# First attention of a two-layer model: 256-column score and value products in three float32r passes, single key/value buffers, normalisation and query parts on GpSimd

## What is computed

```python
# x: 4 x 256 x 256, normalised first; 16 heads of 128
q = (x @ Wq + bq).reshape(b, h, t, dh)
k = (x @ Wk + bk).reshape(b, t, h, dh).transpose(0, 2, 3, 1)
v = (x @ Wv + bv).reshape(b, t, h, dh).transpose(0, 2, 1, 3)
logits = jnp.einsum('bhtd,bhds->bhts', q, k) * scale
mask = jnp.triu(jnp.full((t, t), -jnp.inf, dtype=x.dtype), k=1)
weights = jax.nn.softmax(logits + mask, axis=-1)
out = jnp.einsum('bhts,bhsd->bhtd', weights, v)
out = out.transpose(0, 2, 1, 3).reshape(b, t, h * dh)
return out @ Wo + bo
```

## Time and profile before

| what | value |
|---|---|
| median of 3 runs | 483.01 us (482.86 to 483.03) |
| the profiled execution | 482.84 us |
| its span, first to last instruction | 481.1 us |
| busy: TensorE, VectorE, ScalarE, GpSimd | 456.8, 287.8, 212.8, 56.8 us |
| granted TensorE clock, mean | 1.000 |
| the loop over the units, first scores to the first work after it | 91.67 to 288.55 us |

### The profile page before, as it was taken

How to read it: one execution, slowest core, us unless ns; L and a number is a source line. 1 busy time by engine, 2 the same in 40 slices (tenths; PEclk the granted TensorE clock), 3 DMA queues, 4 the chain that set the end, 5 groups by cost and what they waited for, 6 DMA issues and landing times.

```text
span 481.1 us, 8091 instructions
## 1 busy us (share of the span) xinstructions
PE 456.8 (95%) x2946; PEld 389.0 (81%) x2946; DVE 287.8 (60%) x851; ACT 212.8 (44%) x554; POOL 56.8 (12%) x93
## 2 busy tenths in 40 slices
PE   3999999899999999999999899999998899999997
PEld 2788888698989889898998779999986646658897
DVE  5646574657676667676666547576888753544111
ACT  3454631356565665656555765333161242241100
POOL 3050000000000000000000000111650189200000
PEclk9999999999999999999999999999999999999999
DMA  6910520101010100100000000000899089900011
GB/s 188 227 45 1 176 72 17 44 1 46 0 45 3 43 2 16 30 1 1 1 1 1 2 1 0 1 1 1 280 283 278 3 233 294 256 1 2 0 42 46
DMA packets 40439, 32.32 MB, mean 67 GB/s; under 512 B 6432, under 2 KB 38864, under 8 KB 40400
## 3 DMA queue, kind: packets, MB, share of 16 engines
q1 hardware_dynamic: 40400, 31.80, 23.9%
HBM read 30.75 MB, written 1.05 MB: 66 GB/s over the span
## 4 chain that ended last, share of the span: by engine, by line
PE 83%; DVE 7%; ACT 5%; issue 3%; POOL 1%; DMA 1%; ACTq 0%; DVEq 0%; POOLq 0%
PE bank L779 15%; PE bank L780 15%; PE bank L781 15%; PE bank L947 5%; PE bank L929 5%; PE bank L1154 4%; PE bank L936 4%; PE bank L948 3%; PE bank L928 2%; PE bank L1126 2%; PE bank L1085 2%; PE bank L1146 2%; PE bank L1192 2%; PE bank L1191 2%; PE bank L1189 1%
## 5 line engine op out<-in xcount | busy, mean ns | idle before, releaser
L617 ACT ACTIVATE arena<-arena,nmax 128x128 f32<-128x128 f32 x64 | 25.7, 402 | 77.6 <-DVE nmax L1356 77.0
L779 PE MATMUL bank<-XTl,WA 128*128 128x512 f32 x128 | 54.2, 423 | 3.0 <-POOL WA L480 1.7
L780 PE MATMUL bank<-XTh,WA 128*128 128x512 f32 x128 | 51.4, 402 | 0.0
L781 PE MATMUL bank<-XTh,WA 128*128 128x512 f32 x128 | 51.3, 401 | 0.0
L497 POOL TENSOR_TENSOR arena<-arena 128x256 f32<-128x256 f32 x20 | 16.6, 857 | 266.8 <-ACT arena L680 247.2
L947 PE MATMUL bank<-arena 128*128 128x256 f32 x128 | 39.5, 391 | 1.1 <-ACT arena L626 1.1
L1345 DVE COPY arena<-bank 128x512 f32<-128x512 f32 x32 | 22.1, 691 | 30.6 <-PE bank L781 30.6
L1342 DVE TENSOR_SCALAR arena<-bank,VC 128x512 f32<-128x512 f32 x32 | 23.8, 749 | 24.9 <-PE bank L781 24.9
L779 PE MATMUL bank<-WA,XTh 128*128 128x256 f32 x128 | 38.3, 299 | 0.0
L929 PE MATMUL bank<-arena 128*128 128x256 f32 x128 | 38.2, 380 | 0.0
L780 PE MATMUL bank<-WA,XTl 128*128 128x256 f32 x128 | 35.7, 279 | 0.0
(11 more groups left out here) (273 smaller groups left out, 1193.7 us busy)
## 6 DMA issues: line engine op xcount, KB each, us to landing
arena<-in_L_ffn_Wg SPq DMA_DIRECT2D x6, 704.0 KB, 8.6
arena<-in_L_ffn_Wu SPq DMA_DIRECT2D x6, 704.0 KB, 10.4
arena<-in_L_ffn_Wd SPq DMA_DIRECT2D x6, 512.0 KB, 8.4
arena<-in_L_attn_Wq SPq DMA_DIRECT2D x4, 512.0 KB, 6.9
arena<-in_L_attn_Wk SPq DMA_DIRECT2D x8, 256.0 KB, 2.8
arena<-in_L_attn_Wv SPq DMA_DIRECT2D x8, 256.0 KB, 3.3
arena<-in_L_attn_Wo SPq DMA_DIRECT2D x1, 2048.0 KB, 9.6
arena<-in_L_ffn_Wd SPq DMA_DIRECT2D x6, 192.0 KB, 7.9
```

The costliest lines, as they stand in the source:

```text
L617: nc.scalar.activation(Pb[i][:, 0:128], Pb[i][:, 0:128], ACT.Exp, bias=nmax[:, i, 0:1], scale=-1.0, accum_out=psumr[:, i, 0:1])
L779: pe.matmul(dst, wh, xl, start=start, stop=False)
L780: pe.matmul(dst, wl, xh, start=False, stop=False)
L781: return pe.matmul(dst, wh, xh, start=False, stop=stop)
```

## The change

The 256-column score product and the 256-column value product go through `mm3`; the two 128-column ones stay f32. For this, keys and values are kept as a high part, a low part and a plain f32 part (`KH`, `KL`, `KP`, `VH`, `VL`, `VP`), and as these take more room there is one place for each instead of two. The fills of a pair come in another order (`FILL`, with the last quarter of the keys at the end), and six are done ahead instead of eleven. Waits on keys and values are counted per piece (`KC`). A key fill is emptied by ScalarE (`key_high`, 512 columns) and two VectorE passes, a value fill by three VectorE passes. The transposed probabilities are copied by ScalarE in two pieces and get a low part on VectorE (`t_low`). VectorE keeps the reciprocal (`inverse_sums`); the multiplications go to GpSimd (`normalise`), which also splits the 128 queries that see 256 keys (`query_parts`). Pieces of Wo and of the output projection move to later turns, and the split outputs get a place more (`o_place`). The diff, cut to its core:

```diff
-WO_AT = [16, 19, 22, 26, 53, 55, 57, 59]
-O_AT = {56: 0, 58: 2, 62: 1}
+WO_AT = [16, 19, 22, 26, 58, 59, 60, 61]
+O_AT = {58: 0, 61: 2, 62: 1}
+FILL = (0, 1, 2, 4, 5, 6, 7, 3)
+KC = {f: i + 1 for i, f in enumerate(FILL)}
...
-AHEAD = 11
+AHEAD = 6
...
-        KT = KTf.rearrange("p (a h n) -> p a h n", a=2, h=2)
+        KP = region(20480, 1024).rearrange("p (h b n) -> p h b n", h=2, b=B)
+        KH, KL = (nc.alloc_sbuf_tensor_at(f"K{i}", [P, 2, N], FR, offset=at0 + 4 * (21504 + 2048 * i)) for i in range(2))
         XN = KTf[:, 0:2048].rearrange("p (j d) -> p j d", j=NT)
-        WXA = KTf[:, 2048:4096].rearrange("p (j d) -> p j d", j=NT)
+        WXA = [region(28672 + D * j, D) for j in range(6)] + [region(32768 + D * j, D) for j in range(2)]
-        V = Vf.rearrange("p (a j n) -> p a j n", a=2, j=NT)
+        VH, VL = (nc.alloc_sbuf_tensor_at(f"V{i}", [P, B, 2 * DH], FR, offset=at0 + 4 * (25600 + 1024 * i)) for i in range(2))
+        VP = region(27648, 1024).rearrange("p (b n) -> p b n", b=B)
...
-        PTb = region(29440, 768).rearrange("p (i n) -> p i n", i=2)
+        PTH, PTL = (nc.alloc_sbuf_tensor_at(f"PT{i}", [P, 2, T], FR, offset=at0 + 4 * (29440 + 512 * i)) for i in range(2))
+        PTP = region(30464, 256).rearrange("p (i n) -> p i n", i=2)
+        QH, QL = (nc.alloc_sbuf_tensor_at(f"Q{i}", [P, 2, P], FR, offset=at0 + 4 * (30720 + 256 * i)) for i in range(2))
...
+        OSX = nc.alloc_sbuf_tensor_at("OSX", [P, 2, H // 2, P], FR, offset=at0 + 4 * 16384)
+        def o_place(n):
+            if n == 0:
+                return OSX
+            while n > 4:
+                n = {5: 2, 6: 1, 7: 3}.get(n, n - 4)
+            return OS[:, {2: 1, 1: 0, 3: 3, 4: 2}[n]]
...
+            def query_parts(u):
+                _, _, b, h = unit(u)
+                q = QO[:, h, b, 128:256]
+                if u >= 2:
+                    pool.wait_ge(s_S, u - 1)
+                pool.tensor_copy(QH[:, u % 2], q).then_inc(s_q1, 1)
+                pool.wait_ge(s_q1, u + 1)
+                pool.tensor_tensor(QL[:, u % 2], q, QH[:, u % 2].bitcast(F32), ALU.subtract).then_inc(s_qh, 1)
+            def normalise(u):
+                i = u % 3
+                pool.wait_ge(s_ri, u + 1)
+                pool.tensor_scalar(Pb[i][:, 0:128], Pb[i][:, 0:128], rinv[:, i, 0:1], None, ALU.mult)
+                pool.tensor_scalar(Pb[i][:, 128:384], Pb[i][:, 128:384], rinv[:, i, 1:2], None, ALU.mult).then_inc(s_p, 1)
+            pool.wait_ge(s_qa, 16)
+            pool.wait_ge(s_qd, 16)
             pool.wait_ge(s_xa, NT)
+            for u in range(4):
+                query_parts(u)
+            normalise(0)
+            normalise(1)
+            for u in range(UNITS):
+                if u + 2 < UNITS:
+                    normalise(u + 2)
+                if u + 4 < UNITS:
+                    query_parts(u + 4)
+            pool.wait_ge(s_qc, 1)
             pool.memset(region(30720, 512), MASKED).then_inc(s_pad, 1)
...
+            def key_high(n):
+                p, f = n // 8, FILL[n % 8]
+                if f >= 4:
+                    return
+                hh, half = f // 2, f % 2
+                act.wait_ge(s_kf, n + 1)
+                if p >= 1:
+                    act.wait_ge(s_S, 8 * (p - 1) + 4 * hh + 2 * half + 2)
+                nc.scalar.activation(KH[:, hh, 512 * half:512 * half + 512], pb[6 + n % 2][:], ACT.Identity,
+                                     bias=VC[:, 16 + 2 * p + hh:17 + 2 * p + hh]).then_inc(s_kh, 1)
+            for n in range(3):
+                key_high(n)
             for f in range(4):
                 act.wait_ge(s_wxt, f + 1)
                 nc.scalar.activation(WXT[:, f // 2, 512 * (f % 2):512 * (f % 2) + 512], pb[4 + f % 2][:], ACT.Copy).then_inc(s_wxc, 1)
-            act.wait_ge(s_kv, 96)
-            w_high(6, KVR.rearrange("p a c n -> p (a c n)"))
...
                 act.wait_ge(s_T, u + 1)
                 if u >= 2:
                     act.wait_ge(s_O, u - 1)
-                nc.scalar.activation(PTb[:, u % 2], pb[2 + u % 2][:, 0:384], ACT.Copy).then_inc(s_Tc, 1)
+                nc.scalar.activation(PTH[:, u % 2], pb[2 + u % 2][:, 0:256], ACT.Copy)
+                nc.scalar.activation(PTP[:, u % 2], pb[2 + u % 2][:, 256:384], ACT.Copy).then_inc(s_Tc, 1)
...
+                if u + AHEAD < UNITS:
+                    key_high(u + AHEAD)
+                if u % 8 == 2 and u // 8 + 2 < PAIRS:
+                    act.wait_ge(s_kv, 32 * (u // 8 + 3))
+                    w_high(4 + u // 8 + 2, KVR.rearrange("p a c n -> p (a c n)"))
...
             def scores(u):
                 p, hh, b, h = unit(u)
-                if u % 8 == 0:
-                    pe.wait_ge(s_kc, 8 * p + 4)
+                pe.wait_ge(s_kc, 8 * p + KC[2 * hh + b // 2])
+                pe.wait_ge(s_qh, u + 1)
                 if u >= 2:
                     pe.wait_ge(s_m, u - 1)
-                s, k = pb[u % 2], KT[:, p % 2, hh]
-                pe.matmul(s[:, 0:128], QO[:, h, b, 0:128], k[:, T * b:T * b + 128], start=True, stop=True)
-                pe.matmul(s[:, 128:384], QO[:, h, b, 128:256], k[:, T * b:T * b + 256], start=True, stop=True).then_inc(s_S, 1)
+                s, i = pb[u % 2], u % 2
+                pe.matmul(s[:, 0:128], QO[:, h, b, 0:128], KP[:, hh, b], start=True, stop=True)
+                mm3(s[:, 128:384], QH[:, i], QL[:, i], KH[:, hh, T * b:T * b + T], KL[:, hh, T * b:T * b + T],
+                    True, True).then_inc(s_S, 1)
             def turn(u):
                 pe.wait_ge(s_p, u + 1)
                 if u >= 2:
-                    pe.wait_ge(s_Tc, u - 1)
+                    pe.wait_ge(s_Tl, u - 1)
                 for i in range(3):
                     ins = pe.transpose(pb[2 + u % 2][:, P * i:P * i + P], Pb[u % 3][:, P * i:P * i + P], ident[:])
                 ins.then_inc(s_T, 1)
             def heads(u):
                 p, hh, b, h = unit(u)
-                pe.wait_ge(s_Tc, u + 1)
-                if u % 8 == 0:
-                    pe.wait_ge(s_kc, 8 * p + 8)
+                pe.wait_ge(s_Tl, u + 1)
+                if hh == 0:
+                    pe.wait_ge(s_kc, 8 * p + KC[4 + b])
                 if u >= 2:
                     pe.wait_ge(s_Oc, u - 1)
-                o = pb[4 + u % 2][:, 0:256]
-                pe.matmul(o, V[:, p % 2, 2 * b, P * hh:P * hh + P], PTb[:, u % 2, 0:256], start=True, stop=False)
-                pe.matmul(o[:, 128:256], V[:, p % 2, 2 * b + 1, P * hh:P * hh + P], PTb[:, u % 2, 256:384],
-                          start=False, stop=True).then_inc(s_O, 1)
+                o, i, ds = pb[4 + u % 2][:, 0:256], u % 2, slice(P * hh, P * hh + P)
+                mm3(o, VH[:, b, ds], VL[:, b, ds], PTH[:, i], PTL[:, i], True, False)
+                pe.matmul(o[:, 128:256], VP[:, b, ds], PTP[:, i], start=False, stop=True).then_inc(s_O, 1)
...
-            FIRST_OUT = {54: lambda: out_small(0, 0), 55: lambda: out_small(0, 1),
-                         56: lambda: out_small(1, 0), 57: lambda: out_small(1, 1),
-                         58: lambda: out_heads(0, 0), 59: lambda: out_heads(0, 1),
-                         60: lambda: out_heads(2, 0), 61: lambda: out_heads(2, 1)}
+            FIRST_OUT = {58: lambda: (out_small(0, 0), out_small(0, 1)), 59: lambda: (out_small(1, 0), out_small(1, 1)),
+                         60: lambda: out_heads(0, 0), 61: lambda: out_heads(0, 1),
+                         62: lambda: out_heads(2, 0), 63: lambda: out_heads(2, 1)}
...
             def fill_copy(n):
-                p, f = n // 8, n % 8
+                p, f = n // 8, FILL[n % 8]
+                bank = pb[6 + n % 2]
                 dve.wait_ge(s_kf, n + 1)
-                if f == 0 and p >= 2:
-                    dve.wait_ge(s_S, 8 * (p - 1))
-                if f == 4 and p >= 2:
-                    dve.wait_ge(s_O, 8 * (p - 1))
-                if f == 0 and p == 1:
-                    dve.wait_ge(s_wxt, 4)
-                if f == 0 and p == 0:
+                if n == 0:
                     dve.wait_ge(s_xb, NT)
                 if f < 4:
-                    hh, ts = f // 2, slice(512 * (f % 2), 512 * (f % 2) + 512)
-                    nc.vector.tensor_scalar(KT[:, p % 2, hh, ts], pb[6 + n % 2][:], VC[:, 16 + 2 * p + hh:17 + 2 * p + hh],
-                                            None, ALU.add).then_inc(s_kc, 1)
+                    hh, half = f // 2, f % 2
+                    ts, bias = slice(512 * half, 512 * half + 512), VC[:, 16 + 2 * p + hh:17 + 2 * p + hh]
+                    dve.wait_ge(s_kh, 4 * p + (0, 1, 2, 3)[f] + 1)
+                    nc.vector.tensor_scalar(KP[:, hh, 2 * half:2 * half + 2], bank[:].rearrange("p (b s n) -> p b s n", b=2, s=2)[:, :, 0],
+                                            bias, None, ALU.add)
+                    nc.vector.scalar_tensor_tensor(out=KL[:, hh, ts], in0=bank[:], scalar=bias, in1=KH[:, hh, ts].bitcast(F32),
```

(74 more changed lines are left out.)

1 line of the change is left out of this document (removed).

## The result

The changed kernel takes 557.6 us, the median of four runs (554.79 to 564.26), against 482.9 us in the same session: 1.153 times as long [1.150, 1.156]. Executions over 1.5% above the fastest of their kernel, here the one of 564.26 us, count in the medians but not in the ratios. The forecast was 527 us in 512 to 552. Slower was right, but the time lies above the whole range. The case that came true is the first rival, GpSimd decides (0.21, 534 to 572 us).

What follows compares the result with a forecast made beforehand. TensorE, busy 95% of the span, was taken as the bound. The attention section's +49.2 us and -5.4 ahead of it gave net +43.8 on 482.84, so 526.6, said as 527 us, range 512 to 552.

Steps and rivals of the forecast that it cites:

- the first rival, GpSimd decides: Attention loop: with GpSimd's own time over 2.0 us a turn, its ring is the longer; 534 to 572 us, chance 0.21.
- two rings would close: Attention loop, every turn: one wait cycle through VectorE and ScalarE, one through GpSimd, both longer than TensorE's 2.87 us.
- Vector/scalar ring of 3.56 and 3.70: Attention loop: masking, exponentials, probability copies, `t_low`, fill copies, next masking; 3.56 us with value fills, 3.70 with key fills.
- The 3.77 that the sum used for key turns: Attention loop: 3.77 us per key turn, as the fill itself arrives late when both rings act together.
- GpSimd's ring: Attention loop: scores, masking, reciprocal, `normalise`, `query_parts`, next scores; 1.66 us plus GpSimd's own time, 3.56 us in all.
- G = 1.9, "the middle": GpSimd's own time per loop turn for `normalise` and `query_parts`, taken as 1.9 us between 1.53 and 2.21.
- the upper bound: GpSimd's time per turn with all passes at two-input prices: 1.22 + 0.99 = 2.21 us, for turns up to 3.87.
- Masking 3 to masking 63: Main stretch of the attention loop, summed at 230.4 us from fill turns, weight splits, Wo pieces and late turns.
- The start: -5.4 forecast: Before the loop: five fills and some idle time leave, expert turns wait longer, last copies lose cover; net -5.4 us.
- The end: Masking 63 to the first work after the loop: 9.8 us, against 6.0 in the kernel before.
- TensorE stays the bound: Rival for the attention loop: the vector queue is not held and the change pays; about 474 us, chance 0.05.
- The clock: Rival: TensorE idles over 20% of each turn and its clock falls to 1.2 GHz; about 647 us, chance 0.02.

## Why the prediction was wrong in size

Point by point, by its own steps:

- **What bounded the kernel before, and that two rings would close: right.** Turns left TensorE's 2.87 for a ring in every unit.
- **Vector/scalar ring of 3.56 and 3.70: right but for 0.1.** With GpSimd out of the way it reads 3.45 and 3.83 to 3.84, one below and one above, and over eight turns the two errors cancel, by luck. The 3.77 that the sum used for key turns comes near by luck too: the late fill that it rests on is not there, and the copies are dearer than summed. Each edit that shortens GpSimd's ring alone gives 525 to 531 us, the forecast's 526.6 us.
- **G = 1.9, "the middle": the step that failed.** By the starts in the timeline of the value turn it is 0.58 + 0.87 + 0.38 + 0.46 = 2.29. The query halves cost 0.84, as taken (0.82 to 0.99). The two multiplications cost 1.45, where the upper bound (two-input prices, 0.740 and 0.476) allows 1.22 at most. The bound rested on the belief that a pass with one full input cannot cost more than one with two. Here it costs half as much again as the two-input form of the same work (1.54 against 1.02 busy). The remainder of the ring was summed at 1.66 and measured 1.77. So the sum 1.66 + 1.9 = 3.56, which only tied with the other ring, should have been 1.77 + 2.29 = 4.06, and this ring decides. The forecast had named GpSimd pieces over 2.2 us a turn as a sign that it is wrong. (Two slips in its sums change nothing: half of the two-input step is 0.13, not 0.11, and the parts behind the loop add up to 9.7, not 9.8.)
- **In microseconds.** Masking 3 to masking 63 took 256.0 us against 230.4: 25.6 of the 28.2 us by which the profiled execution missed 526.6. Most of it comes from the ordinary turns: eight of them with one `w_low` took 33.8 us and were summed at 30.5, 24 us over 58 turns. The last two turns of the stretch, with late pieces of Wo and of the output projection, took 9.3 and were summed at 8.1. Putting GpSimd's multiplications behind the query halves removes 28.6 us, and cheapening them by 0.53 us a unit 27.0, so the cause is shown and not only argued.
- **The Trainium skill's rule** (GPSIMD Engine Reference, Engine selection: one-input passes at roughly line rate) had pointed to a G near the lower bound. The copy agrees with it: 293 ns for 128 columns, near and near the 287 ns of VectorE's `tensor_scalar` of 128 columns in the kernel before. The multiplication by a pointer does not: 606 ns for the same 128.
- **The start: -5.4 forecast, -3.5 measured** (scores 0 at 88.13). The wait ahead of the experts' transposes was to grow by 0.9 and grew by 1.2 (0.77 to 1.96), and a halved clock behind it was not foreseen. Scores 0 to masking 3 took 6.56, not 5.9, again with GpSimd's passes in it.
- **The end: right.** Masking 63 to the first work after the loop 9.96, forecast 9.8. What follows it took 192.4 us, as before (192.6).
- **TensorE stays the bound:** false for this order. With the rings opened and the pieces spread it comes true, at 468 us against the 474 that the rival gave.
- **The clock:** 0.994 in the profiled execution, not a fall to 1.2 GHz. In 108 to 340 us TensorE was busy for 170.7 of 232 us and the granted clock read 1.00.

## What to carry to other kernels

When a change puts new steps on engines that run in order, write down every ring from an instruction to the same instruction of the next turn, through queue order as well as data, and give each its length. The longest decides, opening another is worth nothing by itself, and the order of two calls may be worth more than the arithmetic that they hold. If two rings come out equal and one rests on an operation that no row shows, the forecast is a coin toss, and the range has to lean to the side of that operation. A bound by "the nearest dearer operation" holds only if the same form of instruction has been seen on that engine. Where it hasn't, measure the form or write the pass in the form that is known.
